# Products of B and C in the state-space heads: three fp32r products of split halves in place of one fp32 product

## The reference

```python
proj = x @ W_in.T
val, gate, Bp, Cp, dt = jnp.split(proj, ...)      # Bp, Cp: 32 heads x 128
...
CB = jnp.einsum('blhn,bmhn->bhlm', C_c, B_c)
M = CB * jnp.exp(diff)                            # diff: differences of cumulated decays, causal
Y = M @ val_ch + (part carried from earlier chunks) + Dh * val_ch
Y = Y * jax.nn.silu(gate)
return Y @ W_out.T
```

## Time and profile before

| what | value |
|---|---|
| median of three runs | 1694.6 us (1692.33 to 1703.74) |
| profiled execution, its own time | 1694.59 us |
| its span | 1692.8 us |
| mean granted clock of PE | 0.869 of full speed |
| PE busy | 72% of the span |
| DVE, ACT, POOL busy | 55%, 36%, 17% |
| `stage_ssm_heads`: first and last projection start | 937.7 us, 1511.7 us |

### The profile page before, as it was taken

One profiled execution on the slowest core, in us unless ns is written; L12 is line 12 of the kernel. 1 busy time (PEld: TensorE's weight loads), 2 busy tenths in 40 slices (PEclk: granted clock), 3 DMA queues, 4 the chain that ended last, 5 costly groups with the idle time before them and its releaser, 6 DMA issues. The chain is left out here.

```text
span 1692.8 us, 24296 instructions
## 1 busy us (share of the span) xinstructions
PE 1219.3 (72%) x8677; PEld 1001.7 (59%) x8678; DVE 930.1 (55%) x2016; ACT 610.9 (36%) x1445; POOL 293.9 (17%) x314
## 2 busy tenths in 40 slices
PE   2636898465858777001574899999999999987394
PEld 1524666353748766001453688888888888866184
DVE  4645777636615544336563665666665666653435
ACT  3102333411223322004233455555555555532533
POOL 3000000232750000673000601400400230001101
PEclk9877989757979989555797899999999999998597
DMA  5583533030238987330221622421332152200101
GB/s 222 208 218 107 161 103 73 2 136 34 97 118 327 334 300 260 115 105 9 82 99 56 166 75 65 123 88 57 117 91 87 57 136 71 71 18 1 53 1 50
DMA packets 105228, 189.99 MB, mean 112 GB/s; under 512 B 12278, under 2 KB 58614, under 8 KB 102518
## 3 DMA queue, kind: packets, MB, share of 16 engines
q1 hardware_dynamic: 98972, 171.76, 31.6%
q0 software_dynamic: 6144, 16.79, 3.1%
HBM read 123.03 MB, written 65.27 MB: 111 GB/s over the span
## 5 line engine op out<-in xcount | busy, mean ns | idle before, releaser
L1650 ACT ACTIVATE decay<-masked,negcum 128x128 f32<-128x128 f32 x512 | 188.0, 391 | 275.0 <-DVE mixT L1676 266.7
L1676 DVE TENSOR_TENSOR mixT<-pcb,decay 128x384 f32<-128x384 f32 x256 | 130.7, 552 | 68.7 <-PE pcb L1598 67.0
L1699 DVE COPY cT<-pcT 128x512 f32<-128x512 f32 x128 | 88.3, 690 | 127.7 <-PE pcT L1585 127.7
L1596 PE MATMUL pcb<-cT,bT 128*128 128x256 f32 x512 | 153.0, 380 | 0.0
L271 PE MATMUL turned<-ident,xn 128*128 128x128 f32 x96 | 26.5, 434 | 165.0 <-ACT xn L231 140.3
L271 PEld LDWEIGHTS turned<-ident,xn 128*128 128x128 f32 x96 | 17.2, 217 | 173.8 <-ACT xn L231 145.8
L1585 PE MATMUL pbT<-xh,wh 128*128 128x512 f32 x256 | 111.8, 437 | 11.2 <-POOL wl L1558 10.4
L621 ACT ACTIVATE probT<-pst 128x384 f32<-128x384 f32 x128 | 61.6, 491 | 146.6 <-PE pst L561 141.5
L1598 PEld LDWEIGHTS pcb<-cT,bT 128*128 128x128 f32 x512 | 96.8, 189 | 13.7
L1585 PE MATMUL pbT<-xh,wl 128*128 128x512 f32 x256 | 101.9, 398 | 0.0
L1665 DVE TENSOR_TENSOR masked<-cumrow,mask 128x512 f32<-128x512 f32 x128 | 91.3, 714 | 19.1 <-DMA cumrow<-ssm_cum 19.1
(11 more groups left out here) (255 smaller groups left out, 3147.1 us busy)
## 6 DMA issues: line engine op xcount, KB each, us to landing
cumrow<-ssm_cum SPq DMA_DIRECT2D x128, 256.0 KB, 3.3
slots_in<-blank SPq DMA_DIRECT2D x16, 1024.0 KB, 7.0
xg<-slots_in SPq DMA_DIRECT2D x32, 512.0 KB, 5.6
slots_out<-yg SPq DMA_DIRECT2D x32, 512.0 KB, 4.0
stack<-qk_parts SPq DMA_DIRECT2D x32, 384.0 KB, 4.8
wring<-in_expert_quads SPq DMA_DIRECT2D x16, 768.0 KB, 7.7
wring<-in_expert_w SPq DMA_DIRECT2D x64, 192.0 KB, 3.2
wraw<-in_w_bc SPq DMA_DIRECT2D x32, 256.0 KB, 2.8
```

The lines of the kernel that those rows point to most:

```text
L1596: nc.tensor.matmul(pcb[n % 2][q][:, 0:S], bT[:, n % 2, o:o + P], cT[:, n % 2, o:o + S], start=True, stop=True)
L1650: last = nc.scalar.activation(decay[:, n % 2, q, lo:lo + P], masked[:, n % 2, q, lo:lo + P], ACT.Exp, bias=bias)
L1676: last = nc.vector.tensor_tensor(mixT[:, n % KEEP, q, :], pcb[n % 2][q][:], decay[:, n % 2, q, :], ALU.mult)
L1699: nc.vector.tensor_copy(cT[:, n % 2, :], pcT[:]).then_inc(c_out, 1)
```

## The change

The fp32 product of `bT` and `cT` is replaced by three fp32r products. For that, both are split into a rounded high part and the remainder. DVE writes `ch` out of PSUM in place of `cT` (a copy that rounds), waits for its own write, and subtracts it from PSUM into `cl`. ACT still copies `pbT` to `bT`, which is now one deep; POOL makes `bh` out of it by adding zero, and `bl` by subtracting (`low`, two instructions of 128x512 a step). POOL's stream is written in another order: the splits of weights and the copies of values now stand between the steps' `low`. PE's `products` has twelve matmuls, and waits for `b_low` and `c_low` in place of `b_out` and `c_out`; C of the next step also waits for `c_low`. ACT's copy of B of step n waits for `b_low` of n-1. `CUMS` goes from 6 to 4.

```diff
-CUMS = 6
+CUMS = 4
...
-        bT = sb("bT", [P, 2, CHUNK])
-        cT = sb("cT", [P, 2, CHUNK])
+        bT = sb("bT", [P, CHUNK])
+        bh, bl, ch, cl = (sb(name, [P, 2, CHUNK], F32R) for name in ("bh", "bl", "ch", "cl"))
...
@@ gpsimd
-                for b in range(NC):
-                    for j in range(PER):
-                        split(b, j)
-                    for half in range(2):
...
+                def low(n):
+                    pool.wait_ge(b_out, n + 1)
+                    if n >= 2:
+                        pool.wait_ge(cb_done, n - 1)
+                    nc.gpsimd.tensor_tensor(bh[:, n % 2, :], bT[:], none[:].broadcast_to([P, CHUNK]),
+                                            ALU.add).then_inc(b_high, 1)
+                    pool.wait_ge(b_high, n + 1)
+                    nc.gpsimd.tensor_tensor(bl[:, n % 2, :], bT[:], bh[:, n % 2, :].bitcast(F32),
+                                            ALU.subtract).then_inc(b_low, 1)
...
+                split(0, 0)
+                for n in range(HEAD_STEPS):
+                    b, c, j = place(n)
+                    if n + 1 < PER:
+                        split(0, n + 1)
+                    low(n)
+                    if n == 2:
+                        half_values(0, 0)
+                        half_values(0, 1)
+                    if c == NCH - 1 and b + 1 < NC:
+                        split(b + 1, j)
+                        if j == PER - 1:
+                            half_values(b + 1, 0)
+                    if b and c == 0 and j == 2:
+                        half_values(b, 1)
@@ tensor, products
-                    pe.wait_ge(b_out, n + 1)
-                    pe.wait_ge(c_out, n + 1)
+                    pe.wait_ge(b_low, n + 1)
+                    pe.wait_ge(c_low, n + 1)
...
+                    terms = ((bh, ch), (bh, cl), (bl, ch))
                     for q in range(BPC):
                         o = q * S
-                        nc.tensor.matmul(pcb[n % 2][q][:, 0:S], bT[:, n % 2, o:o + P], cT[:, n % 2, o:o + S],
-                                         start=True, stop=True)
-                        last = nc.tensor.matmul(pcb[n % 2][q][:, S:REACH], bT[:, n % 2, o + P:o + S],
-                                                cT[:, n % 2, o + P:o + S], start=True, stop=True)
+                        for lo, hi, col in ((0, S, 0), (P, S, S)):
+                            for m, (key, query) in enumerate(terms):
+                                last = nc.tensor.matmul(pcb[n % 2][q][:, col:col + hi - lo],
+                                                        key[:, n % 2, o + lo:o + lo + P],
+                                                        query[:, n % 2, o + lo:o + hi],
+                                                        start=(m == 0), stop=(m == len(terms) - 1))
...
-                            pe.wait_ge(c_out, n)
+                            pe.wait_ge(c_low, n)
@@ scalar
-                    if n >= 2:
-                        act.wait_ge(cb_done, n - 1)
-                    nc.scalar.activation(bT[:, n % 2, :], pbT[:], ACT.Copy).then_inc(b_out, 1)
+                    if n >= 1:
+                        act.wait_ge(b_low, n)
+                    nc.scalar.activation(bT[:], pbT[:], ACT.Copy).then_inc(b_out, 1)
@@ vector
-                    nc.vector.tensor_copy(cT[:, n % 2, :], pcT[:]).then_inc(c_out, 1)
+                    nc.vector.tensor_copy(ch[:, n % 2, :], pcT[:]).then_inc(c_out, 1)
+                    dve.wait_ge(c_out, n + 1)
+                    nc.vector.tensor_tensor(cl[:, n % 2, :], pcT[:], ch[:, n % 2, :].bitcast(F32), ALU.subtract
+                                            ).then_inc(c_low, 1)
```

More of the change, by code:

```diff
@@ L1499, in stage_ssm_heads @@
         b_out, c_out, dec_masked, dec_out = (chip.sem(n) for n in ("b_out", "c_out", "dec_masked", "dec_out"))
+        b_high, b_low, c_low = chip.sem("b_high"), chip.sem("b_low"), chip.sem("c_low")
         cb_done, mix_out = chip.sem("cb_done"), chip.sem("mix_out")
@@ L1565, in values, with half_values @@
                                           ).then_inc(v_ready, 1)
-                for b in range(NC):
-                    for j in range(PER):
-                        split(b, j)
-                    for half in range(2):
[L1571 to L1576, removed]
+                def low(n):
[7 more added lines that the diff above has]
+                                            ALU.subtract).then_inc(b_low, 1)
+                def half_values(b, half):
+                    if b == 0:
+                        pool.wait_ge(zeros_set, 1)
+                    else:
+                        pool.wait_ge(y_done, (b - 1) * 2 * NCH + 2 * (NCH - 1) + half + 1)
+                    for j in range(half * GROUPS, (half + 1) * GROUPS):
+                        values(b, j)
+                split(0, 0)
[13 more added lines that the diff above has]
+                        half_values(b, 1)
             @block.tensor
```

## The result

The changed kernel takes 1753.28 us, the median of four runs (1748.52 to 1763.16), against 1695.92 us before: 1.034 times as long, with a 95% interval of 1.028 to 1.040. The forecast was 1748. The profiled execution took 1748.52 us, its span is 1746.7 us, 53.9 more than before. Of these, 48.7 lie between the first and the last projection of B (620.3 us against 571.6), 2.6 ahead of the first and 2.6 behind the last.

The account below looks back on a forecast made before the run. The prediction took TensorE to bound the heads' stage, and POOL where weights are split. PE 14, first chunk 7 and block ends 32 made 53 us on 1694.59: 1748 us, the forecast's own range 1731 to 1760.

Parts of the forecast that it names:

- TensorE sets the pace, and three fp32r products don't shorten it: In the heads' stage PE is the bound; twelve fp32r matmuls cost 1.42 us a step against 1.31 before.
- PE's step grows by 0.11 us: PE's term: the twelve fp32r matmuls lengthen each of 128 steps, +14 us in all.
- The 1.31 us removed: Cost of a step's four fp32 products, taken as the 4.08 us step less twelve equal projections.
- products to next projection 1.42 us: Sign of being right on PE: time from a step's first product to its next projection.
- The 128-column price: On PE, a 128-column fp32r matmul was taken to cost 0.118 us, like one of 256 columns.
- four passes: Rival on PE: short fp32r matmuls take four cycles a column, 0.21 us each; 1807 us, chance 0.15.
- First chunk, +7: Stage's first chunk: POOL's `low` pairs beside weight splits and values do not fit, +7 us.
- Block ends, 3 x 10.5 = 32: Last chunks of blocks 0, 1, 2: POOL's two pairs a step 8.4 us, SP's queue 2, each; +32 us.
- DVE's subtraction at nothing: DVE's added 0.69 us a step fills the 0.62 us it waited for products; counted at nothing.
- CUMS at nothing by itself: No term for CUMS alone; two fewer `cumrow` DMAs ahead were named within SP's 2 us a block.
- The masks beside POOL: DVE's masks, 1.02 us otherwise, wait about 0.7 us for POOL in an ordinary step, hidden under 4.61 us.
- the rival that said so: POOL holds up both masks every step, so DVE needs 5.0 to 5.1 us a step; 1786 us, chance 0.14.

Follow-up runs that it names:

- e1: Kernel before with TensorE's part alone: B and C rounded once to fp32r, three fp32r products of high parts, no low parts; 1702.6 us, ratio 1.004.
- e10: e1's kernel with every 256-column product cut into two of 128 columns, 18 matmuls a step; 1810.7 us, a single run on a slower chip.
- e3: Changed kernel with each weight DMA issued three steps later in SP's stream; 1741.6 us, ratio 1.026.
- e6: e3's kernel, with ACT writing B's high part from PSUM so that POOL only subtracts; 1724.2 us, ratio 1.016.
- e7: e1's kernel plus DVE's splitting of C, with its wait and CUMS 4; B not split; 1707.6 us, ratio 1.008.
- e8: Kernel before with CUMS 4 in place of 6 and nothing else; 1698.5 us, ratio 1.002.
- e9: Same kernel as e11, run on the slower chip; ratio 0.988 to the kernel before there.
- e11: Changed kernel with fp32r for 256-column products only, fp32 for 128, later weight DMAs, DVE's finishing in two steps, values' copies spread; 1691.0 us, ratio 0.998.

## Why the prediction was right

- *TensorE sets the pace, and three fp32r products don't shorten it.* Right; e1 shows it alone. The size was too large: the term "PE's step grows by 0.11 us" is 0.05, +14 us is 6. I had taken 0.118 us from twelve equal 256-column matmuls for the short ones too; in the mixed row the mean is 0.110. The 1.31 us removed was no distance of rows 3 either: from the first product to the next projection they give 1.23, so the sign "products to next projection 1.42 us" was set against the wrong yardstick. Measured, it went from 1.23 to 1.32.
- *The 128-column price.* The earlier trace rows were read as a floor of some 256 cycles, and not as four passes, because of the load's length at two clocks. The price holds: e10's 0.109 us for 128 columns is 262 cycles at 2.4 GHz, where four passes would be 512. That the load makes this floor is still argued from its length.
- *First chunk, +7.* Measured 45.11 - 36.24 - 0.67 = 8.2, with 1.5 us of scatter in the 36.24.
- *Block ends, 3 x 10.5 = 32.* Measured 10.6, 9.4 and 10.7 over ordinary chunks, 30.7. The size was right, and the split nearly so: 8.4 were put on POOL and 2 on SP's queue; e3 takes 2 to 3 away by the queue, e6 6.4 by POOL, and 1.2 stay.
- *DVE's subtraction at nothing.* Wrong by a little: 5 us between e1 and e7, 2 of them in ordinary chunks (16 x 0.14) and 2 in the first, which is within its scatter. The last sign of being wrong, PE idle in ordinary steps, did not show: the trace has no idle time of PE there, though such a chunk is 0.30 us longer than in e1.
- *CUMS at nothing by itself.* Right (e8). It was named beside the queue as "two fewer ahead"; that part does nothing before, and was not tried alone in the changed kernel.
- *The masks beside POOL.* In three of the eight steps of an ordinary chunk of the changed kernel the first mask takes about 1.43 us in place of 0.68, and both masks about 1.76 in place of 1.02, as foreseen ("about 0.7 of waiting"). With POOL idle, in e7, it keeps 0.68:

```profile
1031.39 1.42 DVE L1692 TENSOR_TENSOR masked<-cumrow,mask 128x512 f32<-128x512 f32 x1
1032.73 0.41 DVE L1694 TENSOR_TENSOR masked<-cumrow,mask 128x256 f32<-128x256 f32 x1
```

DVE did not become the bound there; the rival that said so is refuted by the ordinary chunk of 36.57 us.
- *What made up the sum.* 16 x 0.67 + 8.2 + 30.7 = 49.6 us against 53 forecast and 48.7 measured in the stage (the last chunk has no successor). The other 5.2 us of the profiled execution lie outside this stretch. What follows the last projection start is 183.5 us before, 186.1 after, and 182.0 to 188.8 in the experiments' profiles; B's first projection starts at 937.7 before, at 940.3 after, and at 935.7 to 944.1 in the experiments on the chips of usual speed. Both are the spread of single executions, and no cause was looked for. So it is partly luck that 53 us came so close to the profile's 53.9: PE's term was 8 us too large, about 5 us in ordinary chunks were put at nothing, and 5.2 us are no part of the mechanism.

The Trainium skill's rule, "TensorE: Matmul & The Clock Gate", section "Back-to-back issue gap", 81 ns for a 128-column matmul with its load, would have made PE's term -15 us, as an estimate. e10 measured 109 ns for fp32r. The section "LDWEIGHTS (loading the stationary operand)", columns over 1.2 GHz, gives 107, and that agrees.

## What to carry to other kernels

Before splitting an fp32 product into three fp32r ones, count matmuls and not columns: under 256 columns an fp32r matmul with its own weight load still costs 0.109 us, so three of 128 columns (0.33 us) are dearer than one fp32 matmul (0.22), while three of 256 (0.35) are cheaper than one (0.44). A helper engine that is idle on average can be full for the eight steps that matter; add up its work where its other duty falls. And a DMA that waits for that helper holds up all that is queued behind it, so the waits in the trace can name the data when the helper is the larger cause.

## What the runs showed of the hardware

- fp32r matmuls that each have a weight load of their own come no closer than 0.109 us in the mean at 2.4 GHz: 18 of 128 columns in 1.96 us (e10), 12 mixed ones in 1.32 us (the changed kernel).
- One chip ran the kernel before at 1746.3 us (11 runs, 1726.3 to 1749.8), 50 us more than the others. In e9's profile from it B's first projection starts at 986.6 us in place of 937.7, while the heads' stage is as long as elsewhere. Most of it is one stop in the expert stage, in which PE stands still for 38.1 us (until 485.99 us) and the profile shows nothing that it waits for; e11's profile of the same kernel has no such stop. The cause is open. Comparing stage with stage, and each kernel with before on the same chip, kept it out of the findings.
